# Second half of a vision tower: queries move against standing keys in the causal scores, values on 64-row by 32-column tiles

## What is computed

```python
# 64 images, T = 64 tokens, C = 256, H = 16 heads of hd = 16
qkv = layernorm(h) @ W_attn
q, k, v = split(qkv)                      # heads of 16 channels
att = einsum('bhid,bhjd->bhij', q, k) / sqrt(hd)
att = where(causal, att, -inf)
att = (x > 0 ? x*x + 1 : -100 <= x <= 0 ? 1 - x/100 : 0) / 1000     # polymax, x = att
y = einsum('bhij,bhjd->bhid', att, v) @ W_proj
h = h + y
h = h + ternary_linear(gelu(ternary_linear(layernorm(h), w_up)), w_down)
```

## Time and profile before

| what | us |
|---|---|
| median of 3 runs | 841.56 (840.88 to 843.34) |
| span of the profiled execution | 839.8 |
| PE busy in the span | 726.8 (87%) |
| DVE busy | 650.7 (77%) |
| ACT busy | 406.4 (48%) |
| masks of the second half, L681, 128 products | 21.2 |
| scores of the second half, L687, 1024 records | 39.3 |
| values of the second half, L701, 1024 records | 19.5 |

### The profile page before, as it was taken

The page is one execution under the profiler, slowest core; times in us unless marked ns, Lnnn a source line. Parts: engine busy times, 40 slices in busy tenths (PEclk is TensorE's granted clock), DMA queues, the critical chain, the costliest instruction groups (busy, mean ns, idle before and its releaser), DMA issues.

```text
span 839.8 us, 24754 instructions
## 1 busy us (share of the span) xinstructions
PE 726.8 (87%) x10487; PEld 510.2 (61%) x10487; DVE 650.7 (77%) x1442; ACT 406.4 (48%) x609; POOL 96.6 (12%) x76
## 2 busy tenths in 40 slices
PE   4879999999999999956786889999999988989857
PEld 3456766666676758544474556675667655565634
DVE  7577878787888788687496589988988887675653
ACT  4536464545455454533223473828455471734503
POOL 1201212121203030200000010000101010000000
PEclk9879999999999999977865999999999999997959
DMA  9033202010202001000000000000000000000000
GB/s 309 27 140 110 76 0 75 0 75 0 75 0 75 0 0 66 38 1 1 1 2 1 2 2 27 3 27 2 25 0 0 25 2 27 2 27 2 3 25 27
DMA packets 7531, 27.22 MB, mean 32 GB/s; under 512 B 2480, under 2 KB 3376, under 8 KB 5936
## 3 DMA queue, kind: packets, MB, share of 16 engines
q1 hardware_dynamic: 7472, 26.35, 8.6%
HBM read 22.16 MB, written 4.19 MB: 31 GB/s over the span
## 4 chain that ended last, share of the span: by engine, by line
PE 54%; DVE 24%; issue 10%; ACT 8%; SPq 1%; POOL 1%; DMA 1%; DVEq 0%; POOLq 0%; ACTq 0%
PE PS L374 8%; PE PS L323 6%; PE PS L745 5%; PE PS L385 5%; PE PS L480 4%; PE PS L710 4%; PE PS L364 3%; PE PS L469 3%; DVE mx L1297 3%; DVE Pm L1303 2%; PE PS L426 2%; PE PS L687 2%; ACT w_s L1019 2%; PE PS L701 2%; DVE th L1355 2%
## 5 line engine op out<-in xcount | busy, mean ns | idle before, releaser
L894 ACT ACTIVATE PT<-PS 128x512 f32<-128x512 f32 x64 | 36.7, 596 | 76.6 <-PE PS L469 76.6
L364 PE MATMUL PS<-ident_s,xn 128*128 128x128 f32 x256 | 48.2, 305 | 25.8 <-DVE xn L1218 22.6
L723 PE MATMUL PS<-xT,wqkv_h 128*128 128x512 f16 x256 | 64.0, 397 | 5.5 <-ACT w_s L1019 4.0
L887 ACT ACTIVATE Pm<-Pm 128x1024 f32<-128x1024 f32 x32 | 33.4, 1056 | 54.9 <-DVE Pm L1303 54.9
L323 PE MATMUL PS<-tokW_h,w_s 128*128 128x256 f16 x504 | 58.5, 273 | 0.0
L364 PEld LDWEIGHTS PS<-ident_s,xn 128*128 128x128 f32 x256 | 30.9, 148 | 38.5 <-DVE xn L1218 20.7
L323 PEld LDWEIGHTS PS<-tokW_h,w_s 128*128 128x128 f16 x504 | 48.7, 98 | 5.8
L745 PE MATMUL PS<-tokW_h,work 128*128 128x256 f16 x448 | 51.3, 273 | 0.0
L1297 DVE TENSOR_REDUCE mx<-PS 128x16 f32<-128x1024 f32 x32 | 38.9, 1216 | 15.0 <-PE PS L437 14.8
L374 PE MATMUL PS<-xT,wat_h 128*128 128x512 f16 x192 | 46.2, 400 | 4.5 <-DVE xT L1601 4.5
L723 PEld LDWEIGHTS PS<-xT,wqkv_h 128*128 128x128 f16 x256 | 23.1, 101 | 43.4 <-ACT w_s L1019 16.3
(11 more groups left out here) (240 smaller groups left out, 1627.0 us busy)
## 6 DMA issues: line engine op xcount, KB each, us to landing
work<-in_x SPq DMA_DIRECT2D x7, 1536.0 KB, 6.9
out<-H SPq DMA_DIRECT2D x8, 512.0 KB, 2.6
w_s<-in_w SPq DMA_DIRECT2D x3, 1024.0 KB, 6.9
work<-in_x SPq DMA_DIRECT2D x3, 512.0 KB, 5.7
wup_s<-in_wup SPq DMA_DIRECT2D x1, 1024.0 KB, 5.1
wdn_s<-in_wdn SPq DMA_DIRECT2D x1, 1024.0 KB, 8.2
w_s<-in_tokW SPq DMA_DIRECT2D x3, 256.0 KB, 4.8
wup_s<-in_wqkv SPq DMA_DIRECT2D x1, 768.0 KB, 7.9
```

Of the source, the lines that this page charges most:

```text
L364: m = pe.transpose(PS[:, bank, t * P:(t + 1) * P], xn[:, t, c * P:(c + 1) * P], ident_s[:, :])
L723: m = pe.matmul(PS[:, UP_BANKS[f % 3], :], wup_h[:, c, f * P:(f + 1) * P], part[:, c, :], start=(k == 0), stop=(k == 2 * C - 1))
```

## The change

In the second half alone:

- **Scores.** The keys stand unmasked (kT, the old qT) and the queries move, masked into two copies (qM, the old kM). The products are those of the first layer (image_scores, L437): 32 rows by 64 columns standing, 128 columns moving, on eight tiles at (32i, 64b), b being the image of the tile. The result has the image and key on the partitions, and the head of the pair among the columns.
- **Masks.** Instead of four full products, sixteen with 32 rows and 64 columns at the same eight positions: eight move 256 columns (rows 32 to 63 of the keys), eight move 128 (rows 0 to 31, for the first 32 queries alone). Their standing operand keyb replaces the bf16 identity; the mask's table is cut to three quarters and loaded by eight transfers in the place of one.
- **Values.** A tile takes 32 products in the place of 16: 64 rows (the keys of one image) by 32 columns, 64 columns moving, eight positions at (64b, 32i), two products (e = 0, 1) adding up in the same place. V2 is padded with zeros so that head e fills its own 16 of the 32 columns. Results of image b go to PSUM bank 4 + b; turned reads both banks.
- **V.** B1_v is a plain product: 6 for a tile, 128 x 128 standing and 256 columns moving. One ACT operation of 128 x 512 evicts a pair of tiles.
- **Evictions of queries and keys.** ACT evicts both chunks of the keys (2 operations), and chunk 0 of the masked queries (2 operations). DVE evicts chunk 1 of the queries (2 operations, v_B1), and now waits for the last product of B1_qk (Bq_mm) where it waited for the first chunk of the keys (Bk_mm). For slot 0, ACT does all six and DVE none.
- **Setup.** keyb is built by a memset and two reductions on DVE.

```diff
 def a_B1_k(g):
-    act.wait_ge(Bk_mm, 2 * g + 2)
-    for e in range(2):
-        act.activation(kB[:, 1, :, e, :], PS[:, 5, :]..., scale=par_s[:, 2 + e:3 + e]).then_inc(Bk1_out, 1)
+    for c in range(C):
+        act.wait_ge(Bk_mm, 2 * g + c + 1)
+        act.activation(kT[:, c, :], PS[:, 4 + c, :], ACT.Copy, scale=1 / WS).then_inc(Bk_out, 1)
...
-def a_B1_q(g):
-    for c in range(C):
+def a_B1_q(g, chunks):
+    for c in chunks:
         act.wait_ge(Bq_mm, 2 * g + c + 1)
-        act.activation(qT[:, c, :], PS[:, 7 - c, :], ACT.Copy, scale=1 / WS).then_inc(Bq_out, 1)
+        for e in range(2):
+            act.activation(qM[:, c, e, :], PS[:, 7 - c, :], ACT.Copy, scale=par_s[:, 2 + e:3 + e])\
+               .then_inc((Bq0_out, Bq1_out)[c], 1)
...
 def v_B1(g):
-    dve.wait_ge(Bk_mm, 2 * g + 1)
+    dve.wait_ge(Bq_mm, 2 * g + 2)
     for e in range(2):
-        dve.tensor_scalar(kB[:, 0, :, e, :], PS[:, 4, :]..., par_s[:, 2 + e:3 + e], None, ALU.mult).then_inc(Bk_out, 1)
+        dve.tensor_scalar(qM[:, 1, e, :], PS[:, 6, :], par_s[:, 2 + e:3 + e], None, ALU.mult).then_inc(Bq1_out, 1)
...
 def B2_scores(g, t):
-    for i in range(4):
-        pe.matmul(PS[:, i, hb:hb + 256], identb[:, :], cmaskb[:, :, :], start=True, stop=False, ...)
-    for b in range(2):
-        for c in range(C):
-            for i in range(4):
-                m = pe.matmul(PS[:, i, hb + c * P + b * L:...], kB[r, c, 2 * t + b, :, :], qT[r, c, at:at + L],
-                              start=False, stop=True, tile_position=(32 * i, 0), ...)
-    m.then_inc(Bs_mm, 1)
+    for upper in (True, False):
+        qs = slice(0, L) if upper else slice(0, 32)
+        at = slice(0, L) if upper else slice(L, 96)
+        for b in range(2):
+            for i in range(4):
+                pe.matmul(masked[:, :, qs], keyb[r, int(upper), :], cmaskb[r, :, at], start=upper,
+                          stop=False, tile_position=(32 * i, b * L), ...)
+    image_scores(t, kT, qM, hb).then_inc(Bs_mm, 1)
...
+def B2_values(g, pair):
     for t in (2 * pair, 2 * pair + 1):
         for c in range(C):
-            for b in range(2):
-                for i in range(4):
-                    m = pe.matmul(PS[32 * i:32 * i + 32, bank, to:to + L], V2[:, t, b, 2 * i + c, :, :],
-                                  F[:, t % 2, at:at + L], start=True, stop=True, tile_position=(0, 32 * i))
+            for e in range(2):
+                for b in range(2):
+                    for i in range(4):
+                        m = pe.matmul(PS[32 * i:32 * i + 32, 4 + b, to:to + L],
+                                      V2[rows, t, 4 * i + 2 * c + e, :], F[rows, t % 2, at:at + L],
+                                      start=(e == 0), stop=(e == 1), tile_position=(b * L, 32 * i), ...)
         m.then_inc(Y_mm, 1)
```

More of the change, by code:

```diff
@@ L276, in build @@
                     for i in range(4) for e in range(2)]
+        loads_B += [(cmask_s[32 * i:32 * i + 32, :, 0:L], cmask[32:64, :, :]) for i in range(4)]
+        loads_B += [(cmask_s[32 * i:32 * i + 32, :, L:96], cmask[0:32, :, 0:32]) for i in range(4)]
         loads_experts = [(w1_s, w1), (w3_s, w3)]
@@ L518, in turn2 @@
                 if last:
-                    pe.wait_ge(Bq_out, 2)
+                    pe.wait_ge(Bq0_out, 2)
+                    pe.wait_ge(Bq1_out, 2)
                 else:
@@ L654, in B1_v @@
             def B1_v(g, tiles):
-                halves_ = (x1_hi, x1_lo)
                 for t in tiles:
                     if t == 0:
-                        pe.wait_ge(Bq_out, 2 * g + 2)
+                        pe.wait_ge(Bq0_out, 2 * g + 2)
                     elif t == 2:
[L661 to L664, removed]
-                            for e in range(2):
[L666 to L669, removed]
+                        pe.wait_ge(Bk_out, 2 * g + 2)
+                    rows_product(PS[:, (7, 5)[t // 2], (t % 2) * E:(t % 2 + 1) * E], (x1_hi, x1_lo),
+                                 slice(t * P, (t + 1) * P), wat_h, slice(2 * E, 3 * E), C).then_inc(Bv_mm, 1)
             def B2_scores(g, t):
@@ new lines, in B2_scores @@
+                image_scores(t, kT, qM, hb).then_inc(Bs_mm, 1)
+            def B2_values(g, pair):
+                for t in (2 * pair, 2 * pair + 1):
+                    count = in_reg(pe, TILES * g + t + 1)
+                    pe.wait_ge(setup_v, 1)
+                    pe.wait_ge(f2_ok, count)
+                    for c in range(C):
+                        for e in range(2):
+                            for b in range(2):
+                                for i in range(4):
+                                    rows = slice(b * L, (b + 1) * L)
+                                    at = i * E + c * P + e * L
+                                    to = (t % 2) * P + c * L
+                                    m = pe.matmul(PS[32 * i:32 * i + 32, 4 + b, to:to + L],
+                                                  V2[rows, t, 4 * i + 2 * c + e, :], F[rows, t % 2, at:at + L],
+                                                  start=(e == 0), stop=(e == 1), tile_position=(b * L, 32 * i),
+                                                  skip_group_check=True)
@@ L793, in slot_B @@
                     pe.wait_ge(Bk_out, 2 * g + 4)
-                B2_values(g, 1, 4)
+                else:
+                    pe.wait_ge(h4_ok, 2 * g + 1)
+                B2_values(g, 1)
                 if nxt:
@@ L1064, in _ @@
             a_B1_k(0)
-            a_B1_q(0)
+            a_B1_q(0, (0, 1))
             x4_high(LAST)
@@ L1193, in setup_B @@
                 dve.tensor_copy(cmaskb[:, :, :], cmask_s[:, :, :]).then_inc(setup_b, 1)
+                dve.wait_ge(setup_b, 4)
+                for u in range(2):
+                    dve.tensor_reduce(keyb[:, u, 32 * u:32 * u + 32],
+                                      ident_s[:, :].rearrange("p (b j) -> p j b", j=32), AX.X, ALU.max)\
+                       .then_inc(setup_b, 1)
                 dve.wait_ge(abs_mm, 1)
@@ L1715, in slot_B @@
                     mean_squares(g - 1)
-                turned(g, 0, 4)
+                turned(g, 0)
                 if nxt:
@@ L1736, in slot_B @@
                 stats4(g, 0)
-                turned(g, 1, 4)
+                turned(g, 1)
                 if routed in ("batch", "last"):
@@ L1782, in _ @@
             norm2(LAST)
-            v_B1(0)
             dve.memset(vbuf[:], 0.0).then_inc(V2_zero, 1)
```

76 lines of the change are left out of this document (31 added, 45 removed).

## The result

The changed kernel takes 846.1 us (median of 9 runs, 843.44 to 847.25), the kernel before 842.77 (9 runs): ratio 1.0044, 95% interval 1.0031 to 1.0058. It is 3.3 us slower. The forecast was 837.2, with a range of 831.0 to 844.5. The profiled spans are 842.7 and 839.8. The ratios in this document are taken over all runs of a kernel and of the kernel before beside it, so they are not the ratios of the medians, and they leave out one run of a later kernel (1020.25 us, in a slower state of the chip).

The account below looks back on a forecast made before the run. PE was taken to lead, in a relay with ACT and DVE in every slot. Scores' savings and eviction costs summed to -9.5, three clock falls added 5.1: -4.4 on the median of 841.56, 837.2 us, range 831.0 to 844.5.

Parts of the forecast that it names:

- long before their use: 0: At setup, eight small transfers and two reductions come long before they are needed, so they cost 0.
- I take 0: Second half, values: a pair goes from 64 to 128 records, eight positions work side by side, so nothing is added to 1.10 us.
- the upper bound (+1.1): Values: if each record keeps its 17 ns, a pair takes 2.2 us, +1.1.
- The last rival: Values: records have their own price, 17 ns each; twelve pairs on the path, +13.2 - 9.5 = +3.7, 845.3 without a fall; chance 0.14.
- point of decision, 0.8 a pair: Values: extra cost a pair from which the price by record decides, 9.5 / 12 = 0.8 us.
- Falls: Clock drops to 0.50 over the dense down product after PE's idle time: three in seven slots, 1.7 us each, +5.1.
- Scores: Second half: a pair takes 1.7 us, not 3.18; slot 0 -0.8, slot 1 -1.5, slots 2 to 5 -5.6, slot 6 -1.4.
- Slot 7's pair: Slot 7's scores run at 1.2 GHz, where a pair costs twice: -2.7 us.
- Evictions: ACT's query eviction at second-half entry +0.6 us; v_B1 waiting for queries: slot 0 +1.5, slots 1 and 6 +0.2 each.
- calling slots 2 to 5 free of cost: v_B1's wait for the queries costs 0 there, since a routed product stands between and DVE arrives after the queries.
- -9.5: Forecast sum in us before the clock: scores' savings plus the costs of evictions, with values and setup at 0.

Follow-up runs that it names:

- the test on before: The kernel before, its mask table loaded by eight transfers at the end of the second half's loads instead of one at their head: 842.95 against 840.35 us, ratio 1.0032.

## Why the prediction was wrong, step by step

**Setup, "long before their use: 0". Wrong.** What counted was not when the mask is used but what stands behind its transfers on SP's queue: the patches of slot 2, issued 5.06 later. +2.1 in the trace; 2.6 in the test on before.

**Values, "I take 0". Wrong by 0.5 a pair,** half of the upper bound (+1.1). The row that gave the price was in the argument: 96 grams in 1.18, 12 ns a record. It was used against the 25 ns that the Trainium skill ("TensorE: Matmul & The Clock Gate", section "Wait — 56ns, not 53.3ns?") states as the least start-to-start, and not as a price, 128 x 12 = 1.5. The runs bear out that there is such a floor, for products on separate tiles at 11 to 12 ns, not at 25. The reason given for 0, that the rate grows with the positions, holds until records come every 12 ns. Ten to twelve pairs on the path make 5 to 6 us, the largest miss (slot 0's first pair, at half clock, lost only 0.1). No kernel with the new scores and the old values was run, so this sum rests on the slots above: about 0.5 won in each of slots 3 to 5, where in slot 3 1.51 had reached the down product. The last rival had the mechanism, at 17 ns, too dear; its point of decision, 0.8 a pair without falls, is not reached, but with three falls paid a pair at 0.5 is enough.

**Scores. Right where the clock was full:** 1.70 a pair, V's eviction 0.60, the relu 1.87 after the slot's start against "about 2.0". Slot 7's pair took 2.39 in the place of 5.79, 3.4 saved where 2.7 was taken, with 0.65 of the clock granted (769.40 to 771.70 above).

**Falls. Right in kind and near in size:** four in the place of three, 1.3 each in the place of 1.7, together 5.3 against 5.1. The count of three was a guess between none and seven. Not foreseen: a fall over slot 1's scores, behind a wait of 2.51 (2.17 before, without a fall), where the pair took 483.89 - 481.03 = 2.86 in the place of 1.70; and the fall of slot 5 that went. There PE waits as long as before, but at full clock after it, 3.62 in the place of 5.19:

```profile
717.58 3.62 PE L638 MATMUL PS<-w_s,gT 128*8 128x256 f32 x16 [2.15 <-DVE gT L1584]
```

**Evictions. Right:** +0.6 at entry (4.60 to 5.20 behind), +1.5 in slot 0, +0.1 in slot 1 (6.60 behind before the second pair of values, 6.74 at the projection; +0.2 forecast). But calling slots 2 to 5 free of cost hid that DVE's part could go to ACT, where time was idle.

**The clock at entry,** 2.45, was in no step; 0.9 of it came back before the first scores, when the clock was at full for a product that ran at half before.

The sum with what was measured: -9.5 + 2.1 + 12 x 0.5 + 5.3 is +3.9; the trace has +2.9 and the runs +3.3. That this comes so near is partly luck, since it leaves out terms that cancel: +2.45 and -0.9 at entry, +1.2 in slot 1's scores, -1.6 in slot 5, -0.7 in slot 7 and -0.4 for slot 0's first values. The range failed because the values' bound of +1.1 was left outside it and the transfers had no bound at all.

## What to carry to other kernels

Cost a moved or split transfer by the time its issue takes and by what is queued behind it, not by when its data are needed. When products are cut into more and smaller ones, multiply the count by the shortest spacing that any row of the trace shows, and take that as a floor. And when PE gets faster inside a relay, look at the clock after the new idle time, and at which engine's queue could be emptied into another's idle time: here that won 0.4 to 0.5%, and the products between nothing and 0.4%.

## What the runs showed of the hardware

Records on separate tiles follow each other by 11 to 12 ns at the least at full clock, whether they move 32 or 64 columns in fp32 or 64 in f16; at half clock 128 of them took 1.96, 15 ns each. Issuing eight small transfers took SP 5.63 us, and the transfer behind them was issued that much later. The same wait of 2.15 us in slot 5 was followed by half clock in one kernel and by full clock in the other. In the changed kernel and its variants idle time in pieces of 0.2 to 0.9 us between short products was followed by falls in two to seven slots of seven, and by none where other products filled it. In a loop, PE can stand 1 to 4 us at a time on nothing but its own issue, in the last pass or the last two, while instruction transfers run; it did so with five products more, with 32 fewer, and in one run with none more or less.
